# A four-layer graph network with GRU cells on one core: interleaved start-up loads, the first graph's check moved to the end, and x brought to the transposed state through vector turns and DRAM

## The chip, the core and the metric

The kernel runs on 1 core of one Trainium2 chip. The metric is the device time of one execution in microseconds (us), the median of several. TensorE is called PE here, VectorE DVE, ScalarE ACT, GpSimd POOL, and SyncE, which issues the DMAs, SP.

## What is computed

Eight graphs of 1024 nodes with 128 channels pass four layers each:

```python
for i in range(L):                                   # L = 4
    hw = einsum('bnc,cd->bnd', h, weight[i])
    m  = einsum('bjn,bjd->bnd', adj, hw)             # adj: (8, 1024, 1024), zeros and ones
    h  = gru_cell(m, h, w_ih[i], w_hh[i], b_ih[i], b_hh[i])
out = layernorm(x + h * nodemask)                    # x: (8, 1024, 128)
# gru_cell: r = sigmoid(xr + hr); z = sigmoid(xz + hz); n = tanh(xn + r * hn)
#           h = (1 - z) * n + z * h,  with gx = m @ w_ih.T + b_ih and gh = h @ w_hh.T + b_hh
```

## The kernel before, in words

**Order of the work.** The graphs go in pairs. A pair has eight steps: step g handles layer g // 2 of graph g % 2 of the pair. `pairs` (line 219) writes out the first and the last pair and runs the two in between as a hardware loop. Every engine has its own instruction stream in its own block, written out by hand, and the streams meet only through semaphores; an engine executes in order, so what stands behind a waiting instruction waits too. SP is such a stream: it issues nearly all DMAs, in program order.

**One step on PE.** `aggregate` forms S = (node features) x (adjacency) for the two halves of 512 nodes: 8 blocks x 2 halves x 2 parts (the features are split into a high and a low part) = 32 products of 128x512. `gates` follows for each half: 9 products of the state hT with the hidden weights, then 9 of S with the input weights, 36 for both halves. So a step is 68 products. The product of `weight` and `w_ih` is made once at the start ("joined" weights).

**Layouts.** The state is needed twice: transposed (channels on the partitions: hT, split into hT_hi by ACT and hT_lo by DVE) for the gates, and natural (nodes on the partitions: nat_hi, nat_lo) for the aggregation. From one layer to the next the state goes from hT to the natural layout by a DVE transpose of 32x32 blocks (`turn`, L905) into `turned`, a DMA to a DRAM scratch (`bounce`, L314), a DMA back into `back` (L325) and the two splits. For x the way is the other one: x is loaded in the natural layout into x_in (L356), and PE transposes it: `transpose_x` (L411, 8 transposes for a graph, at the head of steps 0 and 1 of each pair) writes p_tr, `take_xT` on ACT (L659) and DVE (L892) splits it, and POOL adds the two parts to hT (L1248).

**SP's order around a change of pairs.** In step 5: y of graph 0 (x again, for the residual) and x_in of both graphs of the next pair. In step 6: `send_back` of step 5, y of graph 1, and blocks 0 and 1 of the second adjacency of the next pair (`next_adj`, L290). In step 7: `send_back` of step 6, then blocks 2 to 7. In step 0 of the next pair: `send_back` of step 7, whose result the residual (DVE L921) of the second graph takes. An adjacency block is 512 KB; it waits until the block before it in adj_in has been copied by ACT (`take_adj`, L639) and checked.

**The check.** A general path is taken at the end if the adjacency has low mantissa bits. ACT checks a block in 1 instruction (`check_adj`, L644), except the first graph's eight, which DVE checks (L889, with `mask_first`, L970) in the opening.

**The opening.** SP issues 12 weight loads, 3 small ones for biases and mask, x of graph 0, the 8 blocks of its adjacency (L282), x of graph 1 (L283), and then the 8 blocks of graph 1, each when the block before it has been copied and checked (L288). PE transposes the weights and joins them for all four layers, transposes x, and aggregates block by block as ACT hands the blocks over. DVE copies the odd blocks of graph 1 (`take_adj1`, L900).

Of the kernel before, what the change touches and what calls it, by code (L numbers as in the profile page):

```python
# [21 lines left out]
F32 = mybir.dt.float32  # L22
# [12 lines left out]
def gnn_kernel(nc, x, adj, nodemask, weight, w_ih, w_hh, b_ih, b_hh, out):  # L35
# [10 lines left out]
    LOWBITS = 0xFFF  # L46

    ctx = ExitStack()
    with ctx:
# [51 lines left out]
        p_start = [(p_r, p_z), (p_S[0], p_S[1]), (p_hn, p_xn), (p_r, p_z)]  # L101
# [3 lines left out]
        bounce = nc.dram_tensor("bounce", [2, P, H], F32, kind="Internal").ap()  # L105

# [34 lines left out]
        adj1_ready = sem("adj1_ready")  # L141
        low_zero = sem("low_zero")
# [6 lines left out]
        x_tr = sem("x_tr")  # L149
        xT_hi = sem("xT_hi")  # L150
# [24 lines left out]
        low_first = sem("low_first")  # L175
# [10 lines left out]
        low_masked = sem("low_masked")  # L186
# [29 lines left out]
        x_v = x.rearrange("b (j p) c -> b p j c", p=P)  # L216
        out_v = out.rearrange("b (j p) c -> b p j c", p=P)
# [33 lines left out]
        def wait_adj(eng, graph, j, graph1=False):  # L251

            if graph1:
                if j % 2:
                    eng.wait_ge(adj1_ready, j // 2 + 1)
                else:
                    eng.wait_ge(adj_ready, NB + j + 2)
            else:
                eng.wait_ge(adj_ready, NB * graph + j + 1)
# [9 lines left out]
        def _(sp):  # L269
            def load_layer(l):  # L270
                sp.dma_start(w_nat[l][:, 0], weight[l]).then_inc(w_in[l], 16)
                sp.dma_start(w_nat[l][:, 1:1 + G], w_ih[l].rearrange("(q p) d -> p q d", p=P)).then_inc(w_in[l], 16)
                sp.dma_start(w_nat[l][:, 1 + G:], w_hh[l].rearrange("(q p) d -> p q d", p=P)).then_inc(w_in[l], 16)

            for l in range(L):
                load_layer(l)
            sp.dma_start(bias_rows[0:L * G], b_ih.rearrange("l (q p) -> (l q) p", p=P)).then_inc(rows_in, 16)
            sp.dma_start(bias_rows[L * G:2 * L * G], b_hh.rearrange("l (q p) -> (l q) p", p=P)).then_inc(rows_in, 16)
            sp.dma_start(mask_rows[0:B * NB], nodemask.rearrange("b (j p) -> (b j) p", p=P)).then_inc(rows_in, 16)
            sp.dma_start(x_in[:, 0], x_v[0]).then_inc(x_loaded[0], 16)  # L280
            for j in range(NB):
                sp.dma_start(adj_in[:, j], adj_v[0, j]).then_inc(adj_loaded[j], 16)  # L282
            sp.dma_start(x_in[:, 1], x_v[1]).then_inc(x_loaded[1], 16)  # L283
            for j in range(NB):

                wait_adj(sp, 0, j)
                sp.wait_ge(adj_checked, j + 1)
                sp.dma_start(adj_in[:, j], adj_v[1, j]).then_inc(adj_loaded[j], 16)  # L288

            def next_adj(p, s, first, blocks):  # L290

                for j in blocks:
                    sp.wait_ge(adj_checked, NB * (2 * p + 1 + s) + j + 1)
                    wait_adj(sp, 2 * p + 1 + s, j, first and s == 0)
                    sp.dma_start(adj_in[:, j], adj_v[2 * p + 2 + s, j]).then_inc(adj_loaded[j], 16)
# [10 lines left out]

            def send_back(p, g, first):

                for h in range(2):
# [6 lines left out]
                    if first and g == 0:  # L316
                        sp.wait_ge(low_first, 1)
# [10 lines left out]
            def body(p, first, last):  # L328
                for g in range(STEPS):
                    if g:  # L330
                        send_back(p, g - 1, first)
                    elif not first:
                        send_back(p - 1, STEPS - 1, False)
                    if g in (2, 3):
                        if not last:
                            next_adj(p, 0, first, range((g - 2) * HB, (g - 1) * HB))
                    elif g == 4:
                        if first:

                            sp.wait_ge(start_tr, L)  # L340
                        else:
                            store(p - 1, 0)
                    elif g == 5:
                        if not first:
                            store(p - 1, 1)
                        load_y(p, 0, first)
                    elif g == STEPS - 2:
                        load_y(p, 1, first)
                    if last:
                        pass  # L350
                    elif g == 5:
                        for s in range(2):

                            sp.wait_ge(x_tr, 4 * p + 2 * s + 2)
                            sp.wait_ge(xnat_lo, 2 * p + s + 1)
                            sp.dma_start(x_in[:, s], x_v[2 * p + 2 + s]).then_inc(x_loaded[s], 16)  # L356
                    elif g == STEPS - 2:
                        next_adj(p, 1, first, range(0, 2))
                    elif g == STEPS - 1:
                        next_adj(p, 1, first, range(2, NB))  # L360
# [22 lines left out]
        def _(pe):  # L383
            pe.wait_ge(ident_made, 1)

            def transpose_weights(l):
                px, ph = p_start[l]
                pe.wait_ge(w_in[l], 48)
                if l == L - 1:

                    pe.wait_ge(start_lo, 1)
# [30 lines left out]
            transpose_weights(1)  # L422
            join_weights(0)
            transpose_weights(2)
            join_weights(1)
            transpose_weights(3)
            join_weights(2)
            transpose_x(0, 0, True)
            join_weights(3)

            pe.wait_ge(start_lo, 2)
# [9 lines left out]
            def aggregate(p, g, first):  # L441
                l, s = divmod(g, 2)
                if first and l == 0:

                    pe.wait_ge(xnat_lo, s + 1)
                    for j in range(NB):
                        wait_adj(pe, s, j, s == 1)
                        for h in range(2):
# [4 lines left out]
                            if j == NB - 1:  # L453
                                last.then_inc(s_done, 1)
                    return
# [100 lines left out]
            def body(p, first, last):  # L556
                for g in range(STEPS):
# [3 lines left out]
                    if g < 2 and not (first and g == 0):  # L561
# [57 lines left out]
        def _(act):  # L619
# [8 lines left out]
            def split_w_hh(l):  # L628
# [4 lines left out]
                copy(wh_hi[:, l], p_start[l][1][:, 0:G * C])  # L633

            def split_joined(l):
                act.wait_ge(start_joined, l + 1)
                copy(wx_hi[:, l], p_start[l][0][:, 0:G * C]).then_inc(start_hi, 1)

            def take_adj(p, s, j, first=False):  # L639

                act.wait_ge(adj_loaded[j], 16 * (2 * p + s + 1))
                copy(adj_hi[:, s, j], adj_in[:, j]).then_inc(adj_ready, 2 if first and s == 1 else 1)

            def check_adj(p, s, j):  # L644

                act.wait_ge(adj_loaded[j], 16 * (2 * p + s + 1))
                act.wait_ge(adj_checked, NB * (2 * p + s) + j)
                nc.scalar.activation(low_words[:, :], adj_in[:, j].bitcast(U16)[:, ::2], ACT.Copy,  # L648
                                     accum_out=low_sums[:, bass.ds(NB * (2 * p + s) + j, 1)]).then_inc(adj_checked, 1)
# [80 lines left out]
            def body(p, first, last):  # L730
                checks = [(p, 1, j) for j in range(NB)] + [(p + 1, 0, j) for j in range(NB) if not last]
                for g in range(STEPS):
# [8 lines left out]
                    if g == 0:  # L741
                        graph_of = (p, 1)
                        places = ((), (0,), (2, 4), (6,)) if first else ((4, 5), (6,), (7,), ())
# [18 lines left out]
                    if l == 0 and not early:  # L762
                        take_xT(p, s)
# [3 lines left out]
                    if 1 <= g <= STEPS - 2:  # L767
                        h_high(p, g - 1, 1)
                    if g == 0:
# [5 lines left out]
                    s_high(p, g, 1)  # L775
                    if early:
                        fill(1)
                    for h in range(2):
# [6 lines left out]
                        if h == 1 and not early:  # L785
                            fill(1)
                        gate(n_sb[:, h], t_sb[:, h], t_add, n_act, ACT.Tanh, bias[:, 0, G * l + 2:G * l + 3], p, k)
                        if h == 0:
                            if 1 <= g <= STEPS - 2:
                                take_back(p, g - 1, 1)  # L790
                            if early:
                                fill(2)
# [4 lines left out]
                    fill(3)  # L797
# [3 lines left out]

            split_w_hh(0)
            split_w_hh(1)
            split_joined(0)
            split_w_hh(2)
            split_joined(1)
            split_x(0, 0, True)
            split_joined(2)
            split_w_hh(3)
            take_adj(0, 0, 0)  # L810
            split_joined(3)
            for j in range(1, NB):
                if j == NB - 2:
                    take_xT(0, 0)
                take_adj(0, 0, j)
# [29 lines left out]
        def _(dve):  # L845
# [5 lines left out]
            nc.vector.memset(low[:, :], 0).then_inc(low_zero, 1)  # L851
            nc.vector.memset(low_sums[:, :], 0.0).then_inc(sums_zero, 1)
            dve.wait_ge(low_zero, 1)
# [6 lines left out]
            def split_weights(l):  # L860
                dve.wait_ge(start_hi, l + 1)
                lo(wh_lo[:, l], p_start[l][1][:, 0:G * C], wh_hi[:, l])
                lo(wx_lo[:, l], p_start[l][0][:, 0:G * C], wx_hi[:, l]).then_inc(start_lo, 1)
# [5 lines left out]
            for l in range(L - 1):  # L869
                copy_weights(l)  # L870
            split_weights(0)
            split_weights(1)
            copy_weights(3)

            nc.vector.tensor_copy(bias[:, :, :].rearrange("p a b -> p (a b)"), p_rows[:, 0:2 * L * G])
            nc.vector.tensor_copy(mask[:, :], p_rows[:, 2 * L * G:2 * L * G + B * NB]).then_inc(rows_out, 1)
            split_x(0, 0)
            split_weights(2)
            split_weights(3)
            dve.wait_ge(rows_out, 1)  # L880
            nc.vector.tensor_tensor(bsum[:, :], bias[:, 0], bias[:, 1], ALU.add).then_inc(rows_out, 1)

            def check_adj(p, s, j, first=False):

                dve.wait_ge(adj_loaded[j], 16 * (2 * p + s + 1))
                if not (first and s == 0 and j == 0):

                    dve.wait_ge(adj_checked, NB * (2 * p + s) + j)
# [418 lines left out]
```

## Time and profile before

| | us |
|---|---|
| median of 3 runs (lowest, highest) | 546.95 (546.69, 547.09) |
| the profiled execution's own time | 549.29 |
| its span, first to last instruction | 547.5 |
| PE busy | 515.9 (94%) |
| DVE busy | 397.9 (73%) |
| ACT busy | 375.4 (69%) |
| POOL busy | 218.8 (40%) |
| mean DMA rate | 148 GB/s |

The table is read so: the span is what the trace covers; the profiled execution lies 2.3 us above the median of the unprofiled runs, and 1.8 us of its own time lie outside its span. Busy is the time in which at least one instruction of the engine ran.

### The profile page before, as it was taken

To read this page: it belongs to the slowest core of one execution; us is meant where nothing else is said; L and a number is where in the kernel's file an instruction comes from. 1 tells how busy PE (TensorE), PEld (TensorE's weight loads), DVE (VectorE), ACT (ScalarE), POOL (GpSimd) and SP (SyncE) were. 2 spreads that over 40 slices of the span, in tenths; PEclk is the share of its full clock that TensorE was granted. 3 is DMA by queue.
4 is the path that set the end of the run, shared out by engine and by line. 5 is a ranking of instruction groups with operands and counts; after the bars stand their busy time and mean duration, and the time that the engine had idled before them with its cause. 6 is when DMAs were issued, how large, how long until landed. Compare 5 with 4: busy or idle time off the path is not lost.

```text
span 547.5 us, 7461 instructions
## 1 busy us (share of the span) xinstructions
PE 515.9 (94%) x2288; PEld 420.4 (77%) x2288; DVE 397.9 (73%) x695; ACT 375.4 (69%) x616; POOL 218.8 (40%) x161
## 2 busy tenths in 40 slices
PE   5898999999999999999999999999999999999950
PEld 4566888888888888788888888888888788888740
DVE  3997767666689786666699886666779886666666
ACT  2855777747786787875886877874886677664422
POOL 0034344443245554333345644233354545244332
PEclk9999999999999999999999999999999999999995
DMA  7952256164662165373662156365472122323302
GB/s 225 389 215 77 88 210 222 53 179 136 199 222 78 62 227 196 109 215 117 196 248 75 59 209 214 111 187 158 134 270 81 55 77 78 116 93 123 108 25 80
DMA packets 79808, 80.93 MB, mean 148 GB/s; under 512 B 3656, under 2 KB 63648, under 8 KB 79776
## 3 DMA queue, kind: packets, MB, share of 16 engines
q1 hardware_dynamic: 79504, 80.41, 44.6%
q8 instruction: 16, 0.26, 0.2%
q10 hardware_dynamic: 272, 0.13, 0.1%
q14 instruction: 16, 0.13, 0.1%
HBM read 60.08 MB, written 20.45 MB: 147 GB/s over the span
## 4 chain that ended last, share of the span: by engine, by line
PE 78%; DVE 9%; DMA 5%; issue 3%; ACT 3%; SPq 2%; POOL 1%; DVEq 0%; ACTq 0%; POOLq 0%
PE p_S L472 34%; PE p_r L482 5%; PE p_r L486 5%; PE p_r L483 5%; PE p_z L482 5%; PE p_z L486 5%; PE p_z L483 5%; PE p_hn L482 2%; PE p_hn L483 2%; PE p_hn L486 2%; PE p_xn L486 2%; PE p_xn L482 2%; PE p_xn L483 2%; DMA bounce<-work 2%; DMA adj_in<-in_adj_dram 2%
## 5 line engine op out<-in xcount | busy, mean ns | idle before, releaser
L1256 POOL TENSOR_TENSOR work<-hT,work 128x512 f32<-128x512 f32 x63 | 87.5, 1390 | 259.8 <-ACT work L676 259.8
L472 PE MATMUL p_S<-adj_hi,nat_hi 128*128 128x512 f32 x480 | 187.4, 391 | 0.0
L472 PE MATMUL p_S<-adj_hi,nat_lo 128*128 128x512 f32 x480 | 186.8, 389 | 0.0
L472 PEld LDWEIGHTS p_S<-adj_hi,nat_hi 128*128 128x128 f32 x480 | 90.1, 188 | 18.9 <-DVE nat_lo L848 0.3
L472 PEld LDWEIGHTS p_S<-adj_hi,nat_lo 128*128 128x128 f32 x480 | 90.1, 188 | 18.5
L1137 DVE SCALAR_TENSOR_TENSOR work<-p_hn,bias,work 128x512 f32<-128x512 f32 x62 | 46.5, 749 | 79.4 <-ACT work L676 79.2
L1260 POOL TENSOR_TENSOR work<-work 128x512 f32<-128x512 f32 x63 | 90.4, 1434 | 4.9
L676 ACT ACTIVATE work<-p_r,bsum 128x512 f32<-128x512 f32 x63 | 43.3, 687 | 63.2 <-PE p_r L486 61.9
L676 ACT ACTIVATE work<-work,bias 128x512 f32<-128x512 f32 x63 | 45.7, 726 | 41.5 <-DVE work L1141 36.2
L905 DVE STREAM_TRANSPOSE work<-hT 128x512 f32<-128x512 f32 x62 | 69.1, 1114 | 2.1
L621 ACT ACTIVATE adj_hi<-adj_in 128x1024 fp32r<-128x1024 f32 x60 | 60.3, 1050 | 0.5 <-DMA adj_in<-in_adj_dram 0.4
L964 DVE TENSOR_TENSOR hT<-work 128x512 f32<-128x512 f32 x63 | 43.3, 688 | 22.7 <-POOL work L1260 22.7
L648 ACT ACTIVATE low_words<-adj_in 128x1024 bf16<-128x1024 uint16 x56 | 58.7, 1048 | 1.0
L621 ACT ACTIVATE S_hi<-p_S 128x512 fp32r<-128x512 f32 x64 | 37.8, 591 | 28.2 <-PE p_S L472 23.3
L848 DVE TENSOR_TENSOR S_lo<-p_S,S_hi 128x512 fp32r<-128x512 f32 x64 | 43.3, 677 | 6.9 <-ACT S_hi L621 6.9
L1141 DVE TENSOR_TENSOR work<-p_xn,work 128x512 f32<-128x512 f32 x62 | 42.9, 692 | 6.5
L676 ACT ACTIVATE work<-p_z,bsum 128x512 f32<-128x512 f32 x64 | 44.1, 689 | 0.0
L1248 POOL TENSOR_TENSOR hT<-hT_hi,hT_lo 128x512 f32<-128x512 f32 x16 | 21.7, 1380 | 47.7 <-DVE hT_lo L848 47.7
L848 DVE TENSOR_TENSOR hT_lo<-hT,hT_hi 128x512 fp32r<-128x512 f32 x48 | 33.1, 689 | 6.1 <-ACT hT_hi L621 5.8
L621 ACT ACTIVATE hT_hi<-hT 128x512 fp32r<-128x512 f32 x48 | 30.1, 628 | 10.5 <-DVE hT L964 10.4
L848 DVE TENSOR_TENSOR nat_lo<-low,nat_hi 128x512 fp32r<-128x512 f32 x48 | 32.8, 683 | 0.0
L621 ACT ACTIVATE nat_hi<-low 128x512 fp32r<-128x512 f32 x48 | 29.8, 620 | 0.0
(148 smaller groups left out, 925.6 us busy)
## 6 DMA issues: line engine op xcount, KB each, us to landing
adj_in<-in_adj_dram SPq DMA_DIRECT2D x64, 512.0 KB, 6.3
bounce<-work SPq DMA_DIRECT2D x62, 256.0 KB, 2.0
low<-bounce SPq DMA_DIRECT2D x62, 256.0 KB, 2.8
x_in<-in_x_dram SPq DMA_DIRECT2D x8, 512.0 KB, 6.7
y<-in_x_dram SPq DMA_DIRECT2D x8, 512.0 KB, 4.3
out_dram<-y SPq DMA_DIRECT2D x7, 512.0 KB, 4.1
y<-in_L_gnn_w_ih_dram SPq DMA_DIRECT2D x2, 192.0 KB, 3.4
y<-in_L_gnn_w_hh_dram SPq DMA_DIRECT2D x2, 192.0 KB, 4.3
```

Source lines behind the costliest of these rows:

```text
L472: last = nc.tensor.matmul(p_S[h][:, :], part[:, s, j], adj_hi[:, s, j, half(h)], start=(j == 0 and part is nat_hi), stop=(j == NB - 1 and ...
L482: nc.tensor.matmul(bank[:, :], w_h[:, l, cols], v[0], start=start, stop=False)
L483: nc.tensor.matmul(bank[:, :], w_l[:, l, cols], v[0], start=False, stop=False)
L486: return nc.tensor.matmul(bank[:, :], w[0][:, l, q * C:(q + 1) * C], v[1], start=False, stop=stop)
L621: return nc.scalar.activation(dst, src, ACT.Copy)
L648: nc.scalar.activation(low_words[:, :], adj_in[:, j].bitcast(U16)[:, ::2], ACT.Copy, accum_out=low_sums[:, bass.ds(NB * (2 * p + s) + j, 1 ...
L676: nc.scalar.activation(dst, bank, func, bias=b).then_inc(made, 1)
L848: return nc.vector.tensor_tensor(dst, src, hi.bitcast(F32), ALU.subtract)
L905: nc.vector.transpose(turned[:, h].rearrange("p (m j c) -> p m j c", m=Q, j=HB), hT[:, g % 2, half(h)].rearrange("p (j r m) -> p m j r", j ...
L1137: nc.vector.scalar_tensor_tensor(t_sb[:, h], p_hn[:, :], bias[:, 1, G * l + 2:G * l + 3], r_sb[:, h], ALU.add, ALU.mult).then_inc(t_mul, 1)
L1256: nc.gpsimd.tensor_tensor(t_sb[:, h], hT[:, s, half(h)], n_sb[:, h], ALU.subtract).then_inc(d_sub, 1)
L1260: nc.gpsimd.tensor_tensor(t_sb[:, h], z_sb[:, h], t_sb[:, h], ALU.mult).then_inc(d_mul, 1)
```

## The change

**Opening.** x of graph 0 is the first load; the weights of each layer are followed by two adjacency blocks. The weight rows are loaded three to a partition, contiguously, and the splits on ACT and DVE write them back into order with strided views. PE transposes and joins layers 1 to 3 between the blocks of the first aggregation. ACT takes the even and DVE the odd blocks of both graphs of the first pair. DVE no longer checks graph 0; `mask_first` is gone. Graph 1's blocks wait only for the copy of the block before.

**Check.** In the last pair SP loads graph 0's adjacency once more, in the places where the other pairs load that of the next pair, and ACT checks it there. `mask_low` moves from step 4 to step 5.

**x of later pairs.** `transpose_x` is left for the first pair alone, and POOL's additions too. For every other pair, SP loads x with eight consecutive nodes to a partition (steps 1 and 2), DVE turns it into y in steps 5 and 6 (4 transposes of 128x512 for a pair), SP sends it to a DRAM scratch, and brings it back into hT in 4 DMAs of 32 partitions for each graph. The residual's x comes into y after that.

```diff
 # SP
+            def load_rows(p, s, first):
+                if first:
+                    sp.wait_ge(x_tr, 2 * s + 2)
+                sp.wait_ge(xnat_lo, 2 * p + s + 1)
+                sp.dma_start(x_in[:, s], xrows_v[2 * p + 2 + s]).then_inc(xrows_loaded[s], 16)
+            def send_x(p, s):
+                sp.wait_ge(x_turned, 4 * p + 2 * s + 2)
+                sp.dma_start(x_bounce[s], y[:, s].rearrange("p a b -> p (a b)")).then_inc(x_out[s], 16)
+            def bring_xT(s, pairs_out):
+                sp.wait_ge(x_out[s], 16 * pairs_out)
+                for q in range(Q):
+                    sp.dma_start(hT[q * 32:(q + 1) * 32, s].rearrange("r (m f) -> r m f", m=Q),
+                                 x_bounce[s].rearrange("(m r) (q f) -> q r m f", m=Q, q=Q)[q]).then_inc(x_back[s], 16)
...
+                    if g == 0 and not first:
+                        bring_xT(1, p)
+                        sp.dma_start(y[:, 1], x_v[2 * p - 1]).then_inc(y_loaded[1], 16)
+                    if g in (1, 2) and not last:
+                        load_rows(p, g - 1, first)
...
                     elif g == STEPS - 2:
-                        load_y(p, 1, first)
+                        if last:
+                            load_y(p, 1, first)
+                        else:
+                            send_x(p, 0)
+                            load_x(p, 0)
+                            next_adj(p, 1, first, False, range(0, 2))
+                            sp.wait_ge(x_out[0], 16 * (p + 1))
+                            load_y(p, 0, first)
+                    elif g == STEPS - 1 and not last:
+                        send_x(p, 1)
+                        load_x(p, 1)
+                        next_adj(p, 1, first, False, range(2, NB))
+                        bring_xT(0, p + 1)
 # PE
-                    if g < 2 and not (first and g == 0):
+                    if first and g == 1:
                         transpose_x(p, g, first)
 # ACT
-            def take_xT(p, s):
+            def take_xT(p, s, first):
+                if not first:
+                    act.wait_ge(x_back[s], 16 * Q * p)
+                    act.wait_ge(hn_done, HS * (p - 1) + 2 * (STEPS - 2 + s) + 2)
                 for h in range(2):
-                    act.wait_ge(x_tr, 4 * p + 2 * s + h + 1)
-                    copy(hT_hi[:, s, half(h)], flat(p_tr[h])).then_inc(xT_hi, 1)
+                    if first:
+                        act.wait_ge(x_tr, 2 * s + h + 1)
+                    copy(hT_hi[:, s, half(h)], flat(p_tr[h]) if first else hT[:, s, half(h)]).then_inc(xT_hi, 1)
...
-                checks = [(p, 1, j) for j in range(NB)] + [(p + 1, 0, j) for j in range(NB) if not last]
+                checks = [(p, 1, j, first, False) for j in range(NB)]
+                checks += [(p + 1, 0, j, False, last) for j in range(NB)]
 # DVE
+            def turn_x(p, s, n, first):
+                dve.wait_ge(xrows_loaded[s], 16 * (p + 1))
+                if not first:
+                    dve.wait_ge(out_stored[s], 16 * p)
+                rows = slice(n * HB, (n + 1) * HB)
+                nc.vector.transpose(y[:, s].rearrange("p a b -> p (a b)").rearrange("p (q a j) -> p j q a", q=Q, j=NB)[:, rows],
+                                    x_in[:, s, rows].rearrange("p j (q c) -> p j q c", q=Q)).then_inc(x_turned, 1)
...
-            for j in range(NB - 2):
-                check_adj(0, 0, j, True)
-            take_xT(0, 0)
+            split_x(0, 0)
+            copy_weights(0)
+            take_odd(0, 1)
+            take_xT(0, 0, True)
+            split_weights(0)
+            for l in range(1, L):
+                copy_weights(l)
+                if l == L - 1:
+                    take_rows()
+                take_odd(0, 2 * l + 1)
+                split_weights(l)
 # POOL
-                    if l == 0:
+                    if l == 0 and first:
```

## Rows read from the trace of the kernel before

**Rows 1.** Windows: length, busy us of PE, PEld, DVE, ACT, POOL, clock, DMA

```profile
55.64:148.12 92.48, 92.48 (x409) 76.53 (x408) 60.64 (x87) 65.61 (x107) 34.22 (x25) 1.00 0.48 154
```

**Rows 2.** Timeline of PE in the opening: start, length, instruction

```profile
26.40 0.39 PE L482 MATMUL p_r<-hT_hi,wh_hi 128*128 128x512 f32 x1
...
55.64 0.39 PE L472 MATMUL p_S<-adj_hi,nat_hi 128*128 128x512 f32 x1
```

**Rows 3.** Single DMAs of the opening: issue, then time from issue to landing

```profile
L273 SPq DMA_DIRECT2D y<-in_L_gnn_w_hh_dram x1: 488/488/488, 6.3 to 6.3; - x1
...
DMA to landing us min/median/max: 4.2/4.2/4.2
...
L282 SPq DMA_DIRECT2D adj_in<-in_adj_dram x1: 707/707/707, 12.7 to 12.7; - x1
...
DMA to landing us min/median/max: 11.2/11.2/11.2
...
L283 SPq DMA_DIRECT2D x_in<-in_x_dram x1: 628/628/628, 13.5 to 13.5; - x1
...
DMA to landing us min/median/max: 12.2/12.2/12.2
```

**Rows 4.** Timeline of DVE in the opening

```profile
17.39 0.55 DVE L848 TENSOR_TENSOR wx_lo<-p_r,wx_hi 128x384 fp32r<-128x384 f32 x1
...
37.32 0.68 DVE L900 CAST adj_hi<-adj_in 128x1024 fp32r<-128x1024 f32 x1
```

**Rows 5.** Timeline of PE, steps 0 and 1 of pair 1, and the head of pair 3

```profile
148.12 1.03 PE L418 MATMUL p_tr<-ident,x_in 128*128 128x128 f32 x8
...
156.26 0.39 PE L482 MATMUL p_r<-hT_hi,wh_hi 128*128 128x512 f32 x1
...
164.54 1.04 PE L418 MATMUL p_tr<-ident,x_in 128*128 128x128 f32 x8
...
180.87 0.39 PE L472 MATMUL p_S<-adj_hi,nat_hi 128*128 128x512 f32 x1
...
399.51 0.27 PE L418 MATMUL p_tr<-ident,x_in 128*128 128x128 f32 x1
```

**Rows 6.** Block 7 (L295) and the scratch store behind it (L314): issue and landing

```profile
L295 SPq DMA_DIRECT2D adj_in<-in_adj_dram x1: 328/328/328, 149.3 to 149.3; - x1
DMA to landing us min/median/max: 7.7/7.7/7.7
...
L314 SPq DMA_DIRECT2D bounce<-work x1: 326/326/326, 151.3 to 151.3; - x1
DMA to landing us min/median/max: 6.5/6.5/6.5
...
L295 SPq DMA_DIRECT2D adj_in<-in_adj_dram x1: 473/473/473, 400.9 to 400.9; - x1
DMA to landing us min/median/max: 9.6/9.6/9.6
```

**Rows 7.** The page, part 6: DMA issues, size, median us to landing

```profile
bounce<-work SPq DMA_DIRECT2D x62, 256.0 KB, 2.0
low<-bounce SPq DMA_DIRECT2D x62, 256.0 KB, 2.8
...
y<-in_x_dram SPq DMA_DIRECT2D x8, 512.0 KB, 4.3
```

**Rows 8.** Timeline of ACT at the head of pair 1

```profile
153.81 1.06 ACT L621 ACTIVATE hT_hi<-p_tr 128x512 fp32r<-128x512 f32 x2
...
159.25 0.69 ACT L676 ACTIVATE work<-p_r,bsum 128x512 f32<-128x512 f32 x1 [0.56 <-PE p_r L486]
```

**Rows 9.** Timeline of DVE, step 0 of pair 1: second half's gates, residual's second half

```profile
164.21 0.75 DVE L1137 SCALAR_TENSOR_TENSOR work<-p_hn,bias,work 128x512 f32<-128x512 f32 x1 [0.77 <-ACT work L676]
...
168.37 2.17 DVE L921 SCALAR_TENSOR_TENSOR y<-low,mask,y 128x128 f32<-128x128 f32 x4
```

**Rows 10.** Windows at the end of the program: the granted clock is the seventh number

```profile
535.00:540.00 5.00, 1.11 (x4) 0.67 (x4) 4.86 (x24) 3.00 (x8) 2.34 (x4) 0.50 0.21 61
```

More of the change, by code:

```diff
@@ L278, in _ @@
[L278 to L282, printed above, removed]
+                if l == L - 1:
+                    load_rows()
+                for j in (2 * l, 2 * l + 1):
+                    sp.dma_start(adj_in[:, j], adj_v[0, j]).then_inc(adj_loaded[j], 16)
@@ L762, in body @@
                     if l == 0 and not early:
-                        take_xT(p, s)
+                        take_xT(p, s, first)
                     s_high(p, g, 0)
@@ L784, in body @@
                             take_back(p, g - 1, 0)
-                        if h == 1 and not early:
+                        if early:
+                            fill(1 + h)
+                        elif h == 1:
                             fill(1)
@@ L879, in _ @@
[L879 to L888, printed above, removed]
-                nc.vector.tensor_tensor(low[:, :], low[:, :], adj_in[:, j].bitcast(I32),
-                                        ALU.bitwise_or).then_inc(adj_checked, 1)
@@ L1089, in body @@
             def body(p, first, last):
-                checks = [(0, 0, NB - 2), (0, 0, NB - 1)] if first else []
-                def fill():
-                    if checks:
-                        check_adj(*checks.pop(0))
-                        if not checks:
-                            mask_first()
                 for g in range(STEPS):
@@ L1115, in body @@
                     if l == 0 and not (first and g == 0):
-                        take_xT(p, s)
+                        take_xT(p, s, first)
                     s_low(p, g, 0)
@@ L1119, in body @@
                         h_low(p, g - 1, 1)
+                    if first and g == 0:
+                        s_low(p, g, 1)
                     if g == 0:
@@ L1123, in body @@
                         split_x(p + 1, 0)
-                    fill()
-                    s_low(p, g, 1)
+                    if not (first and g == 0):
+                        s_low(p, g, 1)
                     if not first:
@@ L1150, in body @@
                                 make_shift(p - 1, g - 2)
+                            if g in (STEPS - 3, STEPS - 2) and not last:
+                                turn_x(p, g - (STEPS - 3), 0, first)
                             if last and g == STEPS - 2:
@@ L1168, in body @@
                     if first and g == 0:
[L1169 removed]
+                        take_odd(1, 7)
                     if 1 <= g <= 2 and not first:
                         graph_moments(p - 1, g - 1)
[L1172 to L1173 removed]
+                    if g in (STEPS - 3, STEPS - 2) and not last:
+                        turn_x(p, g - (STEPS - 3), 1, first)
+                    if last and g == STEPS // 2 + 1:
                         mask_low()
[L1176 to L1178 removed]
+            split_x(0, 0)
+            copy_weights(0)
+            take_odd(0, 1)
+            take_xT(0, 0, True)
+            split_weights(0)
+            for l in range(1, L):
+                copy_weights(l)
+                if l == L - 1:
+                    take_rows()
+                take_odd(0, 2 * l + 1)
+                split_weights(l)
+            dve.wait_ge(rows_out, 1)
+            nc.vector.tensor_tensor(bsum[:, :], bias[:, 0], bias[:, 1], ALU.add).then_inc(rows_out, 1)
             pairs(dve, body)
```

196 lines of the change are left out of this document (87 added, 109 removed).

## The prediction

> **What bounds the kernel now.** I read the page first, for which engine is fullest, then windows laid on whole pairs, then the timelines of each engine where one pair ends and the next begins, and last the single DMAs there. From the start of step 2 to the end of the first pair PE is busy in every one of the 92.48 us [rows 1]: the kernel is bound by PE once it runs, at 92.48 / 6 = 15.41 us a step, 0.227 us for each of its 68 products. The other engines have slack, so what the change adds to DVE or ACT costs nothing as long as it is early enough; what it takes from PE counts in full, and what makes PE wait counts in full too. Outside this regime lie the opening, before 55.64 us, and the tail, which is not touched.
>
> **The opening.** Before, the first gates start at 26.40 us and step 2 at 55.64 [rows 2], 29.24 us later. The last weight lands at 6.3 + 4.2 = 10.5 us, block 7 of the first adjacency at 12.7 + 11.2 = 23.9, x of graph 1 at 13.5 + 12.2 = 25.7 [rows 3]. Between 10.5 and 23.9 one x and eight blocks arrive, nine pieces of 512 KB, so one costs 1.5 us, and an x by itself 1.8 us. The change keeps the bytes, but the weights come in longer runs between the blocks. At the rate of blocks their 1.84 MB take 3.5 x 1.5 = 5.2 us, so block 7 lands at about 2 (the first landing; a lone scratch store takes 2.0 [rows 7]) + 1.8 + 5.2 + 8 x 1.5 = 21.0 us. If the layout gains nothing it stays at 23.9. Behind block 7 stand DVE's copy (0.68), two splits (0.55 each [rows 4]) and a small sum: gates at 21.0 + 2.1 = 23.1 instead of 26.40, a gain of 3.3 (0.3 if nothing is gained on landing). From the gates to step 2, PE's own work is 2 x 36 products (16.3), 32 for graph 1 (7.3) and x's transposes, which take 148.12 to 156.26 less 7.25, 0.9 us [rows 5]: 24.5 against 29.24, so 4.7 of stalls can go. They are due to DVE, which loses eight checks and the mask; graph 1's last block would land at 21.0 + 1.8 + 8 x 1.5 = 34.8 and is wanted at 38.5 or so. Total of the opening: -8.0 us, between -5.0 and -8.7.
>
> **Edits that cost nothing.** The eight extra checks stand in the last pair in the slots in which the middle pairs have eight of their own, and their loads likewise; those pairs run at PE's pace. POOL loses 12 additions and was not late. The 12 block transposes of x on DVE (the like of `turn`) fall into steps 5 and 6, behind work whose next input comes from POOL, and one may take as long as a `turn`; without this cover each would be late by its own length for one half's S_lo. The row loads and stores that they need are issued in steps 1, 2 and 6 behind waits that are long met.
>
> **PE's transposes.** Six of the eight go: 6 x 0.9 = 5.3 us from PE. Before, steps 0 and 1 of a pair take 180.87 - 148.12 = 32.75 us [rows 5]; I set zero at the start of a pair (148.12) and compare the two steps with that.
>
> **The new path of x, at the same place.** hT of graph 0 is wanted when the aggregation ends, 7.25 us after zero. `bring_xT(0)` is the last thing SP issues in step 7, behind `send_x(1)`, `load_x(1)` and blocks 2 to 7. What is the queue's state then? Before, block 7 is issued at 149.3 and lands 7.7 later: +9.0 us after zero. At the head of the last pair it is 400.9 + 9.6 = 410.5 against a start of 399.51 [rows 5]: +11.0. The scratch store issued at 151.3 takes 6.5 instead of a median of 2.0 [rows 6, 7] and lands 0.7 behind the block: this queue serves in order of issue. Nobody waits for that store yet, so the backlog is free today. With the change, x for hT sits in that store's place, and PE waits for it. Mean of block 7, counting the first value for the two middle changes as well: (9.0 + 9.0 + 11.0) / 3 = 9.7 us. In front of it come now y of graph 0 (an x: 1.8, 0 if the queue has a gap for it), `send_x` (1.5) and `load_x` (1.8), and the four DMAs themselves (1.5; perhaps 3, each goes to 32 partitions only). So x arrives at T = 9.7 + 6.6 = 16.3 us, with bounds 14.2 and 18.3.
>
> The Trainium skill (DMA: Bandwidth & Descriptors, "Anatomy of one DMA") gives a DMA 2.0 us plus its bytes at 436 GB/s, so 1.2 us for 512 KB in a full queue against the 1.5 of the rows here; by it the four added pieces would be 4.8 us, T 14.5, and the whole sum some 5 us lower.
>
> From T the chain is: ACT, standing in `take_xT`, makes hT_hi, S_hi, two blocks of adjacency, nat_hi and the second S_hi before it may do the sigmoid; from 153.81 to the end of that sigmoid at 159.25 + 0.69 these are 6.1 us [rows 8], 0.5 of it idle: T + 5.6. PE's second half needs this sigmoid to empty p_r and has 18 products: step 0 ends at T + 9.8 (bound by ACT, so that a slow clock after the stall, 0.50, or 1.2 GHz, at the end of the trace after PE had stood idle [rows 10], adds at most 1 us). For the middle pairs SP goes on only when the queue lets it: store and load of the scratch for half 0, half 1 the same, 4 DMAs for graph 1, then y of graph 1. Store lands at T + 0.7, load and second store +3.3, second load issued T + 4.1, the four issues to T + 6, y lands 4.3 later [rows 7]: T + 10.4. DVE stands at the residual for it (before, y was loaded a step earlier). Behind it are queued: the residual's first half (1.1, half of the second's 2.17 [rows 9]), the second half's two gate operations, new state, turn and h_lo of half 0 (from 164.21 to 168.37, less 0.24 idle: 3.9), the residual's second half (2.2), new state and turn of half 1 (1.8 of those 3.9 once more), and only then hT_lo of graph 1 (0.6): T + 20.0. PE wants that at T + 9.8 + 7.25 + 0.5 = T + 17.5. A second stall of some 2.5 us, and step 1 ends at T + 20.0 + 34 products (7.7) = T + 27.7. The price of a change of pairs is T + 27.7 - 32.75 = T - 5.05; the transposes' gain is in it. Without the second stall it is T + 9.8 + 7.25 + 8.15 - 32.75 = T - 7.6.
>
> **Sum.** 3 x (16.3 - 5.05) = +33.7, opening -8.0: +25.7. The profiled execution's own time is 549.29 and its span 547.5; it lies 2.3 above the median of 546.95. The difference carries over to the median: 546.95 + 25.7 = 572.7, rounded to 572. Low end of this case: T = 14.2, no second stall, the best opening: 3 x 6.6 - 8.7 = +11, 558. High end: T = 18.3, opening -5: +34.8, 582, and a few more if each pair starts its successor's loads later, as the last rows (+11.0 after +9.0) hint: 587.
>
> **Rivals.**
> - *The queue absorbs more.* `send_x` and `load_x` fill gaps, T is 12 to 13, the second stall is small: 3 x (12.5 - 6.3) - 8.0 = +10.6, or down to 3 x 4.9 - 8.7 = +6: 553 to 558. For it: four backlog figures are sums, not measured together. Against: the queue held block 7 for 7.7 and 9.6 us [rows 6], so it had no gap. 10%.
> - *x for hT is not held up at all* (the place is `bring_xT(0)`; several transfers share the engines, or the blocks are out earlier because DVE and SP have less in their way). If T is under 6.6, PE gains 0.9 at each of six places and the opening's 8.0: 546.95 - 5.3 - 8.0 = 533.6. It decides at T = 7.6 + 8.0 / 3 = 10.3: below, the kernel is faster than before. Against it stands the store that landed only at +9.7, behind block 7. 9% for all on this side.
> - *The opening does not do what it says*: DMA stays the bound and block 7 lands at 23.9; 3 us more, inside the range. If at the same time T = 10 or so, no change: 2%.
>
> **Chances.** Forecast 79%, with 558 to 587; the first rival 10%, the faster side 9%, no change 2%. A difference under 0.2% (1.1 us) can't be told from none here: the three runs spread by 0.4 us. The range 555 to 587 leaves out the faster side, half of the first rival and a little above. Slower by over 0.2%: 89%.
>
> **What would show it.** PE's waits, now almost empty between 56 and 518 us, should show three of 8 to 11 us on p_r, put down to ACT's hT_hi or the DMA into hT, each at 7 us after the start of a pair, and three of 1 to 4 us on hT_lo a step later; DVE's waits should show y from x at three places. The four DMAs into hT of graph 0 should need 8 us or more to land, those of graph 1 about 3. L418 should count 16 transposes. Step 2 should begin at 47 to 50 us. Wrong would be: the DMAs into hT landing under 4 us after issue with blocks outstanding; or PE busy throughout the head of a pair.

## The result, and the profile after

The kernel with the change takes 584.91 us (median of 4 runs, 582.92 to 590.07) against 547.02 before: 1.069 times as long, 95% interval 1.064 to 1.073. The forecast was 572 within 555 to 587, and slower. The profiled execution's own time is 582.92, its span 581.0.

PE's waits after, from the view of who waited for whom (us in total, times, longest):

```profile
PE p_r L518 <- ACT hT_hi L657: 29.0, 3, 10.4
PE p_tr L575 <- DVE hT L1101: 6.8, 1, 6.8
PE p_r L431 <- DMA work<-in_L_gnn_w_hh_dram: 6.6, 1, 6.6
PE p_r L522 <- DVE hT_lo L890: 5.4, 3, 1.8
PE p_S L508 <- ACT adj_hi L657: 3.4, 3, 1.9
```

The first row is the foretold first stall, three times, 8.7 to 10.4 us; the fourth is the second stall, on hT_lo a step later; the fifth, for blocks of graph 1 that ACT had not yet copied, was not foretold. The second and third stand outside (the tail and the first load).

The timeline of PE at the first change of pairs, which answers to [rows 5]:

```profile
142.41 0.39 PE L508 MATMUL p_S<-adj_hi,nat_hi 128*128 128x512 f32 x1
...
158.53 0.79 PE L518 MATMUL p_r<-hT_hi,wh_hi 128*128 128x512 f32 x1 [8.71 <-ACT hT_hi L657]
...
168.45 0.39 PE L508 MATMUL p_S<-adj_hi,nat_hi 128*128 128x512 f32 x1
...
174.50 0.50 PE L508 MATMUL p_S<-adj_hi,nat_hi 128*128 128x512 f32 x1 [0.90 <-ACT adj_hi L657]
...
179.35 0.50 PE L522 MATMUL p_r<-hT_lo,wh_hi 128*128 128x512 f32 x1 [1.79 <-DVE hT_lo L890]
...
187.19 0.39 PE L508 MATMUL p_S<-adj_hi,nat_hi 128*128 128x512 f32 x1
```

The pair starts at 142.41 without transposes, and its two first steps end at 187.19: 44.8 us, where they took 32.75 before. At the other two changes (starts at 279.96 and 420.27, ends at 327.49 and 467.82) they take 47.5 each. Together that is 41.6 us more than three times 32.75.

The DMAs. These are single issues and their landings: block 7 (L311) at the first change, the last two of the four DMAs into hT of graph 0 (L337), at the first and the last change, and y of graph 1 (L372) at the first:

```profile
L311 SPq DMA_DIRECT2D adj_in<-in_adj_dram x1: 430/430/430, 145.7 to 145.7; - x1
...
DMA to landing us min/median/max: 10.2/10.2/10.2
...
L337 SPq DMA_DIRECT2D hT<-x_bounce x2: 431/432/433, 147.1 to 147.6; - x2
DMA to landing us min/median/max: 10.0/10.0/10.0
...
L337 SPq DMA_DIRECT2D hT<-x_bounce x2: 433/448/462, 426.6 to 427.1; - x2
DMA to landing us min/median/max: 9.6/9.9/10.3
...
L372 SPq DMA_DIRECT2D y<-in_x_dram x1: 421/421/421, 164.5 to 164.5; - x1
DMA to landing us min/median/max: 4.6/4.6/4.6
```

The last of the four is issued at 147.6 and lands 10.0 later: 157.6, so T = 15.2 us after the pair's start; at the last change 427.1 + 10.3 is 17.1 after 420.27, and at the middle one 16.4 (285.9 + 10.5 after 279.96). The mean is 16.2, and the forecast was 16.3. Its parts hold too: block 7 landed 13.5 us after the pair's start (145.7 + 10.2), and 15.3 and 16.0 at the other two changes, 14.9 in the mean against 9.7 + 5.1 = 14.8 in the forecast's sum; hT follows 1.1 to 1.7 behind it (1.5). The shortest of the 24 DMAs into hT takes 3.0.

The second stall is seen in the waits and the timeline of DVE:

```profile
DVE y L953 <- DMA y<-in_x_dram: 10.6, 3, 4.3
```

```profile
169.40 1.37 DVE L953 SCALAR_TENSOR_TENSOR y<-low,mask,y 128x128 f32<-128x128 f32 x4 [3.07 <-DMA y<-in_x_dram]
170.69 0.74 DVE L1153 SCALAR_TENSOR_TENSOR work<-p_hn,bias,work 128x512 f32<-128x512 f32 x1
...
173.90 1.00 DVE L890 TENSOR_TENSOR hT_lo<-hT,hT_hi 128x512 fp32r<-128x512 f32 x1
174.82 2.17 DVE L953 SCALAR_TENSOR_TENSOR y<-low,mask,y 128x128 f32<-128x128 f32 x4
...
177.63 1.10 DVE L937 STREAM_TRANSPOSE work<-hT 128x512 f32<-128x512 f32 x1
178.65 1.26 DVE L890 TENSOR_TENSOR hT_lo<-hT,hT_hi 128x512 fp32r<-128x512 f32 x2
```

This is the foretold order: DVE stands 3.07 us for y, and everything up to hT_lo of graph 1 follows without a gap.

The clock, in windows of two us (length; busy us of PE, PEld, DVE, ACT and POOL; clock; DMA share and GB/s), at the first change and then after the second stall of the middle one:

```profile
154.00:156.00 2.00, 0.00 (x0) 0.00 (x0) 0.00 (x0) 0.00 (x0) 0.00 (x0) 0.63 1.08 269
156.00:158.00 2.00, 0.00 (x0) 0.00 (x0) 0.00 (x0) 0.23 (x1) 0.00 (x0) 0.50 0.70 204
158.00:160.00 2.00, 1.47 (x4) 1.14 (x5) 1.57 (x3) 2.00 (x4) 0.00 (x0) 0.50 0.18 44
160.00:162.00 2.00, 2.00 (x8) 1.58 (x6) 0.33 (x1) 2.00 (x3) 0.00 (x0) 0.66 0.64 223
162.00:164.00 2.00, 2.00 (x10) 1.67 (x9) 1.73 (x2) 1.78 (x4) 0.00 (x0) 1.00 0.41 100
...
319.00:321.00 2.00, 2.00 (x7) 1.54 (x6) 2.00 (x7) 0.00 (x0) 0.00 (x0) 0.50 0.07 21
```

While PE stands idle the clock falls to 0.50 (1.2 GHz), and the first products after the wait run at it: the 36 of step 0 take 168.45 - 158.53 = 9.9 us instead of 8.2. This is no small part of the price. PE's listed waits at the three changes add up to 29.0 + 5.4 + 3.4 = 37.8 us, and 5.3 us of transposes are gone; the two steps are 41.6 us longer all the same. The 9.1 us between lie in time in which PE counts as busy, most of it, as far as the windows show, under the lower clock.

**The opening** gives 5.7 us: step 2 starts at 49.93 instead of 55.64 [rows 2]. The timeline of PE:

```profile
25.35 0.47 PE L518 MATMUL p_r<-hT_hi,wh_hi 128*128 128x512 f32 x1 [1.07 <-DVE wx_lo L890]
...
49.93 0.39 PE L508 MATMUL p_S<-adj_hi,nat_hi 128*128 128x512 f32 x1
```

Balance of the two traces: +41.6 at the changes of pairs, of which 1.9 were there before (at the last change, where the two steps took 434.14 - 399.51 = 34.6), and -5.7 in the opening: +34.0. The spans differ by 33.5.

### The profile page after: what moved, and what is told of

The parts are those of the page before. It is cut to its first block, busy times and chain, and to the rows that moved or that the text cites. A ratio compares the mean times of both kernels' runs of the same rounds, so it can differ in the third digit from the quotient of the medians.

```text
span 581.0 us, 7363 instructions
## 1 busy us (share of the span) xinstructions
PE 517.5 (89%) x2240; PEld 420.5 (72%) x2240; DVE 404.1 (70%) x700; ACT 382.5 (66%) x628; POOL 201.8 (35%) x149
## 4 chain that ended last, share of the span: by engine, by line
PE 63%; DMA 15%; DVE 9%; SPq 4%; issue 4%; ACT 2%; POOL 1%; DVEq 0%; ACTq 0%; POOLq 0%
PE p_S L508 25%; DMA bounce<-work 11%; PE p_r L522 4%; PE p_r L518 4%; PE p_r L519 4%; PE p_z L518 4%; PE p_z L522 4%; PE p_z L519 4%; DMA y<-in_x_dram 3%; PE p_hn L518 2%; PE p_hn L522 2%; PE p_hn L519 2%; SPq L337 2%; DVE y L953 2%; PE p_xn L519 2%
## 5 line engine op out<-in xcount | busy, mean ns | idle before, releaser
L686 ACT ACTIVATE low_words<-adj_in 128x1024 bf16<-128x1024 uint16 x64 | 67.0, 1047 | 1.0
L890 DVE TENSOR_TENSOR hT_lo<-hT,hT_hi 128x512 fp32r<-128x512 f32 x60 | 41.3, 698 | 36.6 <-ACT hT_hi L657 36.3
L657 ACT ACTIVATE adj_hi<-adj_in 128x1024 fp32r<-128x1024 f32 x56 | 56.9, 1047 | 9.3 <-DMA adj_in<-in_adj_dram 9.3
L657 ACT ACTIVATE hT_hi<-hT 128x512 fp32r<-128x512 f32 x60 | 36.9, 625 | 31.7 <-DMA hT<-x_bounce 20.4
L518 PE MATMUL p_r<-hT_hi,wh_hi 128*128 128x512 f32 x64 | 26.5, 414 | 30.1 <-ACT hT_hi L657 29.0
L657 ACT ACTIVATE S_hi<-p_S 128x512 fp32r<-128x512 f32 x64 | 37.5, 587 | 22.8 <-PE p_S L508 17.8
L518 PEld LDWEIGHTS p_r<-hT_hi,wh_hi 128*128 128x128 f32 x64 | 12.3, 192 | 35.2 <-issue 20.6
L953 DVE SCALAR_TENSOR_TENSOR y<-low,mask,y 128x128 f32<-128x128 f32 x56 | 27.7, 553 | 12.9 <-DMA y<-in_x_dram 10.6
```

Of the source, the lines that this page charges most:

```text
L518: nc.tensor.matmul(bank[:, :], w_h[:, l, cols], v[0], start=start, stop=False)
L657: return nc.scalar.activation(dst, src, ACT.Copy)
L890: return nc.vector.tensor_tensor(dst, src, hi.bitcast(F32), ALU.subtract)
```

## The experiments

The theory going in: SP's queue serves in order, so what PE and DVE wait for at a change of pairs comes behind six blocks and the new transfers of x. Its rivals are named in each expectation. "Before" ran beside each group at 546.7 to 548.5.

**The opening alone.** The path of x of before was put back into the changed kernel:

```diff
-                    if first and g == 1:
+                    if g < 2 and not (first and g == 0):
                         transpose_x(p, g, first)
...
-                        send_x(p, 1)
-                        load_x(p, 1)
                         next_adj(p, 1, first, False, range(2, NB))
-                        bring_xT(0, p + 1)
...
-                    if l == 0 and first:
+                    if l == 0:
```

> The change's opening and its moved check, with x of all pairs transposed by PE as before. If the two parts are independent, step 2 begins at 49.9 us instead of 55.6 and the whole is 5.7 us faster than before: 541.3. Rival: the extra adjacency loads and checks of the last pair, or a later wait, eat the gain: 547. The difference of the full change to this run is the price of the path of x.

Measured: 542.35 us, 0.991 of before (0.990 to 0.993), 4.7 us less where 5.7 were expected. The parts add up to within 1 us, and this version is faster than both kernels. PE never waits between the opening and the tail:

```profile
PE p_tr L567 <- DVE hT L1088: 6.8, 1, 6.8
PE p_r L423 <- DMA work<-in_L_gnn_w_hh_dram: 6.8, 1, 6.8
PE p_tr L460 <- DVE hT L983: 2.5, 1, 2.5
PE p_r L510 <- DVE wx_lo L877: 1.2, 1, 1.2
PE p_S L471 <- ACT adj_hi L649: 0.3, 1, 0.3
```

So the eight extra loads and checks in the last pair cost nothing, and the path of x costs 584.91 - 542.35 = 42.6 us.

**Less backlog.**

```diff
+                    if s == 1 and j > 1:
+                        sp.dma_start(adj_in[:, j, 0:N // 4], adj_v[2 * p + 2 + s, j][:, 0:N // 4]).then_inc(adj_loaded[j], 16)
```

> The full change, but blocks 2 to 7 of the second adjacency of a later pair are loaded in their first quarter of columns only (the other columns keep the graph before them, so later graphs are computed with other adjacencies). This leaves out 2.4 MB of the backlog. Theory: the DMAs into hT of graph 0 land 5.8 us sooner, at 9.5 us after the pair's start instead of 15.2, a change of pairs costs that much less, and the time is 565 to 568. Rival, that the way through turns and scratch is slow by itself and the blocks don't matter: 583 to 587.

This kernel leaves out three quarters of blocks 2 to 7, so later graphs are computed with other adjacencies.

Measured: 565.8 (564.2 to 567.4), as expected. The first stall shrinks from 29.0 to 8.2 us:

```profile
PE p_r L521 <- ACT hT_hi L660: 8.2, 3, 3.5
PE p_r L525 <- DVE hT_lo L893: 4.2, 3, 1.8
PE p_S L511 <- ACT adj_hi L660: 3.3, 3, 1.9
```

Only the bytes ahead were changed: the backlog is the cause of 20.8 of the 29.0 us, not the turns or the scratch. Store and load of x and a quarter of the blocks still stand ahead of hT.

**hT first.**

```diff
                     elif g == STEPS - 1 and not last:
+                        bring_xT(0, p + 1)
                         send_x(p, 1)
                         load_x(p, 1)
                         next_adj(p, 1, first, False, range(2, NB))
-                        bring_xT(0, p + 1)
```

> The full change, but the four DMAs into hT of graph 0 are the first thing SP issues in step 7 after the state's way back, ahead of the store and load of x and of blocks 2 to 7. Theory of one queue in order: the first stall (8.7 to 10.4 us, three times) goes, but y for the residual is still issued behind the scratch store that drains behind the blocks, so y lands 27 us after the pair's start as before, hT_lo of graph 1 follows at 37, and step 1 ends at the same 45 us: the time stays at 583 to 588. Rival, that only the wait for hT costs: three times 9.7 less, 555.

Measured: 579.84 (578.85 to 580.82), below the expected 583 to 588. The rival falls: the DMAs into hT now land in 3.4 us (median of all 24), and the time falls by 5 only. But the expected first stall of zero is wrong, for one on hT_hi stays:

```profile
PE p_r L518 <- ACT hT_hi L657: 15.3, 3, 5.7
PE p_S L508 <- ACT adj_hi L657: 15.2, 3, 6.2
```

```profile
ACT adj_hi L657 <- DMA adj_in<-in_adj_dram: 17.6, 6, 6.3
```

ACT copies blocks 0 to 3 of graph 1 at the end of step 7, ahead of `take_xT` in its stream. What hT gained on the blocks, the blocks lost, and ACT stands up to 6.3 us at block 2 with hT already there. The row on adj_hi (15.2 us) is y, as expected, in another place: DVE waits 22.8 us for it in all, ACT waits for DVE's gates, and so copies the last block of graph 1 late. I had ordered SP's queue anew and not looked at who in ACT's stream waits for what is now last.

**y early.**

```diff
-                        sp.dma_start(y[:, 1], x_v[2 * p - 1]).then_inc(y_loaded[1], 16)      # step 0
...
                         bring_xT(0, p + 1)
+                        sp.wait_ge(x_out[1], 16 * (p + 1))
+                        sp.dma_start(y[:, 1], x_v[2 * p + 1]).then_inc(y_loaded[1], 16)      # step 7
```

> The full change, but y of graph 1 is loaded in step 7, when its turned x has left, behind the DMAs into hT of graph 0, instead of in step 0 behind everything. Theory: the first stall stays (9 to 10 us), the residual no longer waits, and the second stall on hT_lo (2.5 us with what surrounds it) goes: three times 3.3 less than the full change, 574 to 577. Rival, that y is not what holds DVE: 585.

Measured: 576.58 (576.02 to 578.28), as expected: the first stall stays, the second nearly goes.

```profile
PE p_r L519 <- ACT hT_hi L658: 30.2, 3, 10.9
...
PE p_r L523 <- DVE hT_lo L891: 1.6, 3, 0.5
```

**Both orders.** The two edits together, with y behind the blocks:

```diff
                     elif g == STEPS - 1 and not last:
+                        bring_xT(0, p + 1)
                         send_x(p, 1)
                         load_x(p, 1)
                         next_adj(p, 1, first, False, range(2, NB))
-                        bring_xT(0, p + 1)
+                        sp.wait_ge(x_out[1], 16 * (p + 1))
+                        sp.dma_start(y[:, 1], x_v[2 * p + 1]).then_inc(y_loaded[1], 16)
```

> The full change with both reorderings: the DMAs into hT of graph 0 first in step 7, y of graph 1 in step 7 behind the blocks. Theory: no first stall; what is left is that the scratch store of step 7 still drains behind store, load, six blocks and y, so the half of the residual that waits for its way back comes some 7 us late and hT_lo of graph 1 is ready 30 us after the pair's start instead of 23: two steps take 38 us instead of 32.75, three times, on top of the opening's 542.4: 557, between 552 and 562. Rival, that the two orders were all that was wrong: 542.4 less PE's 5.3 us of transposes, 537.

Measured: 569.30 (568.35 to 570.61), 12 us above the expectation and outside its range. The miss is again ACT, in the waits of ACT from 120 to 180 us:

```profile
ACT adj_hi L658 <- DMA adj_in<-in_adj_dram: 6.1, 2, 5.9
```

and so 16.0 us of stalls of PE on hT_hi remain (3 times, at most 5.7). The second stall is still there too (5.5 us on hT_lo, 3 times). hT, blocks 2 and 3, and the scratch of step 7 are each wanted within some 8 us, so that none of the orders tried is good for all; that no order is, was not shown. Blocks 2 and 3 ahead of the store and load of x, for one, was not tried.

**The blocks on ACT's queue.** ACT issues the eight blocks itself, each after its own copy; SP's order as in the run before, or that of the change:

```diff
+            def load_second(p, j):
+                act.wait_ge(adj_ready, NB * (2 * p + 2) + j + 1)
+                act.dma_start(adj_in[:, j], adj_v[2 * p + 3, j]).then_inc(adj_loaded[j], 16)
...
                     def fill(n):
+                        while copied:
+                            load_second(p, copied.pop(0))
                         for j in places[n]:
                             take_adj(*graph_of, j, first and g == 0)
+                            if g >= STEPS - 2:
+                                copied.append(j)
```

> As the run before, and the eight blocks of the second adjacency of a later pair are issued by ACT on its own DMA queue, each right after ACT has copied the block before it, so that SP's queue holds nothing large in front of the scratch and hT. Theory: the backlog is gone from the critical queue and the blocks also start some 5 us earlier; no stall of PE at a change of pairs, 542.4 - 5.3 = 537, between 535 and 541. Rivals: the two queues share the same engines and the sum of bytes is what counts: 550 to 557; or ACT, with some 0.4 us for each issue, falls behind: 545 or more.

> The full change in its own order on SP, with only the eight blocks moved to ACT's queue. Theory: the DMAs into hT land about 5 us after the pair's start, before PE wants them; y of graph 1 is still issued last and lands at 15, about 3 us late for DVE, of which little reaches PE: 537 to 543. Rival, that the order on SP matters by itself: 555 or more.

Measured: 553.78 (552.94 to 554.65) and 573.20 (572.4 to 574.86). My theory of one queue in order falls in half. Moving the blocks does help (15.5 us with the new order, 11.7 with the old), but far less than it should: 537 and 537 to 543 were expected. With the new order the first rival, 550 to 557, is right, and with the old one the rival that SP's order matters by itself. The edit also lets the blocks start earlier, each right after its copy, and no run separates this from the second queue. Here are the store and the load of the scratch of step 6 in the first of the two runs, issued while ACT's blocks are under way:

```profile
L350 SPq DMA_DIRECT2D bounce<-work x1: 338/338/338, 131.9 to 131.9; - x1
...
DMA to landing us min/median/max: 4.6/4.6/4.6
...
L361 SPq DMA_DIRECT2D low<-bounce x1: 366/366/366, 136.6 to 136.6; - x1
...
DMA to landing us min/median/max: 6.4/6.4/6.4
```

Before, their medians are 2.0 and 2.8 [rows 7]; nothing else was on its way on SP's queue here. The two queues share the engines, so a small transfer is not held to the end of the backlog, but it is slowed. The Trainium skill (DMA: Bandwidth & Descriptors, "Issuing engines are not separate DMA queues") says that DMAs run on the same 16 engines and interleave whichever engine started them; these rows agree. With the change's own order (573.20) hT was still behind store and load of x, PE's first stall was 5.2 to 5.8 us at each change, and y stayed last (DVE waits 9.5 us for it in all).

**Bytes without waits.** The opening-only kernel with ballast:

```diff
+            def ballast(p, first, n):
+                if not first:
+                    sp.wait_ge(x_back[n] if n < 2 else x_out[0], 16 * p)
+                sp.dma_start(x_bounce[n], wh_hi[:, :, :].bitcast(F32).rearrange("p a b -> p (a b)")[:, 0:N]).then_inc(
+                    x_back[n] if n < 2 else x_out[0], 16)
...
                             next_adj(p, 1, first, False, range(0, 2))
+                            ballast(p, first, 0)
                     elif g == STEPS - 1 and not last:
+                        ballast(p, first, 1)
+                        ballast(p, first, 2)
                         next_adj(p, 1, first, False, range(2, NB))
```

> The opening-only kernel with three stores of 512 KB that nobody waits for (constant weights into a scratch in DRAM), one behind blocks 0 and 1 in step 6 and two ahead of blocks 2 to 7 in step 7: the bytes of the path of x in those places, without its waits. Theory: the queue had only some 2 us of slack before the residual of step 7 is late, so bytes alone cost: the scratch comes back 4.5 us later, DVE is held about 3 and PE about 2 us at each of three changes of pairs: 548.5, between 546 and 552. Rival, that only a transfer somebody waits for costs: 542.4. The gap that remains to the runs with both orders mended says what the bytes do not explain.

Measured: 552.56 (551.61 to 553.79), a little over the range, and 10.2 us above the run without ballast. Each taken against the kernel before beside it (548.54 and 547.08), the difference is 8.8. In the traces the two first steps of a pair take 35.7, 35.2 and 36.6 us instead of 32.7, 32.8 and 33.0, 8.9 together; most of the rest lies in the opening, where nothing was changed (step 2 starts at 50.8 instead of 50.1). So stores that no engine needs cost some 3 us at each change of pairs, because PE then waits for what was already just in time:

```profile
PE p_r L519 <- ACT hT_hi L658: 3.5, 3, 1.7
...
PE p_r L519 <- ACT work L715: 1.5, 4, 0.5
PE p_hn L519 <- DVE work L1149: 1.2, 3, 0.4
```

The way there is not the expected one. DVE stands only 0.5 to 0.8 us for the scratch at each change; it is ACT that stands for blocks 2 and 3 (4.2 us in 6 waits, against 1.3 in 3 without ballast) before it makes hT_hi.

**The opening's miss.**

```diff
-                        pe.wait_ge(start_lo, L)
-                        pe.wait_ge(rows_out, 2)
+                        pe.wait_ge(start_lo, L - 1)
...
+                if not prior:
+                    pe.wait_ge(start_lo, L)
+                    pe.wait_ge(rows_out, 2)
                 product(p_hn, (wh_hi, wh_lo), l, 2, state, True, True).then_inc(hn_done, 1)
```

> The opening-only kernel, with PE's wait for the last layer's split weights and for the biases moved behind the first six products of the first gates (those write banks that are free one layer earlier). Theory: the 1.1 us that PE stands there go, which are half of what the opening gained less than forecast: 541.3. Rival, that ACT or DVE, which make S_hi and S_lo only then, hold PE right after: 542.4 unchanged.

Measured: 542.53 (541.18 to 543.09), 0.990 of the kernel before beside it (0.988 to 0.992), against 0.991 (0.990 to 0.993) without the edit. The wait of 1.1 us on wx_lo is gone from the trace and 0.4 us on ACT come in a little later; the intervals overlap, and whether 0.7 us were won stays open. In the trace the first weights came 0.7 us later (PE waits 7.5 instead of 6.8 for them) and step 2 starts at 51.0 instead of 50.1, which hides a gain of that size: from the last product of the first aggregation to step 2 it is 25.6 us instead of 26.2.

## Why the prediction was right, and where it was off

**Direction and mechanism held, step by step.** PE bound the kernel; the scratch store behind block 7 showed what a transfer in that place would meet; T was forecast at 16.3 and came out at 15.2, 16.4 and 17.1. The last pair's checks cost nothing, as the opening-only run shows, and neither do DVE's turns of x: in the changed kernel PE has no listed wait in steps 2 to 7. The forecast rise was 25.7 us, the measured one 584.91 - 547.02 = 37.9: inside the range, but 12 us off in size.

Two things in its working are not right, though little hangs on them. The bounds of T, 14.2 and 18.3, do not follow from the terms named: 16.3 - 1.8 is 14.5, and 16.3 + 1.5 is 17.8. And "nobody waits for that store yet" was too strong. SP waits for it, and its load feeds the residual; at the last change before, where that store took 8.6 us, ACT stood 1.1 us for it and DVE 0.5 for the load, and the two steps took 34.6 us. The backlog was nearly free, not free, and the ballast run shows how little room there was.

**The first mis-sized term: the end of step 1 at T + 27.7.** Measured are T + 29.6 (44.8 - 15.2), T + 31.1 and T + 30.4, 2.7 more on average, 8 us in three changes. At the first change 1.1 of its 1.9 is y, which landed at T + 11.5 and not T + 10.4: SP issued it at T + 6.9 instead of T + 6, and it took 4.6 instead of 4.3. Most of the rest is DVE's chain, 10.2 us from y to PE's next product on hT_lo instead of 9.6. At the middle change 34 products after the second stall took 327.49 - 318.05 = 9.4 us instead of 7.7: the clock had fallen again (0.50 in the last window row above), after PE had stood for 0.7 and then for 1.8 us. The forecast had allowed for a slow clock after the first stall only. At the last change y landed at T + 12.8.

**The second: the opening, -8.0 forecast, -5.7 measured.** Block 7 was to land at 21.0 and did so at 13.0 + 8.1 = 21.1; from the gates to step 2 the forecast was 24.5 us and it took 24.6. The step that failed is "gates at 23.1", 2.1 us behind block 7: they came at 25.35. I had put only DVE's work behind the block. The last layer's join on PE stands between blocks 6 and 7, and its split goes from PE to ACT to DVE and back; ACT first waited for the mask on DVE. The rows of DVE and ACT there:

```profile
22.35 0.68 DVE L928 CAST adj_hi<-adj_in 128x1024 fp32r<-128x1024 f32 x1
23.93 0.68 DVE L890 TENSOR_TENSOR wh_lo<-p_xn,wh_hi 128x384 fp32r<-128x384 f32 x1 [0.89 <-ACT wx_hi L657]
24.52 0.65 DVE L890 TENSOR_TENSOR wx_lo<-p_hn,wx_hi 128x384 fp32r<-128x384 f32 x1
```

```profile
22.53 0.70 ACT L657 ACTIVATE wh_hi<-p_xn 128x384 fp32r<-128x384 f32 x1 [1.62 <-DVE mask L932]
23.22 0.68 ACT L657 ACTIVATE wx_hi<-p_hn 128x384 fp32r<-128x384 f32 x1
```

With these two terms as measured the forecast's sum is 41.6 - 5.7 = 35.9 instead of 25.7. The median rose by 37.9; the profiled execution of the changed kernel lies 2.0 us below its median, which is the rest. (The 1.9 us of stall at the last change before are about what the profiled execution of before lies above its own median.)

**The rivals.** That the queue absorbs more is out: T was never under 15. The faster side is out by the same number, and the third, that block 7 of the opening lands at 23.9, by its landing at 21.1. Of what the path of x costs, 42.6 us, the bytes alone explain 9 to 10 (ballast) and the two wrong places in SP's order 584.91 - 569.30 = 15.6. The rest, some 17, is argued and not shown by a run of its own: ACT and DVE that wait for blocks and scratch, and the low clock after each wait. y's place alone is worth 8.3 and hT's alone 5.1; the 2.2 us by which both together exceed the sum are too few against the spread of the change's four runs to speak of an interaction. The gain it was paid with is at most 5.3.

**What stays open.** Whether any placement makes the path of x pay. It would have to move its bytes out of the 20 us around a change of pairs, for instance by turning x before step 5; y is in use there as the residual of the pair before, so it needs another buffer, and it was not tried.

## What to carry to other kernels

A transfer that nobody waits for may be late with hardly a trace in the engines' waits; before putting another in its place, look up its time from issue to landing and compare it with the median of its like (here 6.5 against 2.0). Count a moved or added DMA three times: for who waits for it, for what it delays behind it in its queue, and for the bytes that it takes from all queues. And where one queue's order is changed, read the streams of all engines in order for what they now find last.

## What was not expected of the hardware

A second queue was only in part a way round the first: with the blocks on ACT's queue a store of 256 KB took 4.6 us instead of 2.0, and a load 6.4 instead of 2.8; behind blocks on its own queue such a store took 5.6 to 8.6 before. In a full queue a block of 512 KB lands 1.4 us after the one before it (blocks 6 and 7 of the opening in the changed kernel, at 12.3 + 7.4 and 13.0 + 8.1). PE's clock fell not only in waits of 9 us but once (at the middle change) after two waits of 0.7 and 1.8 us that lay 5 us apart, which cost 1.7 us; at the other two changes, after waits of 0.9 and 1.8 and of 1.9 and 1.8 us in the same places, it stayed at 1.00. Why it fell the one time stays open.
